# Second attention: key and query stacks without padding, 32-row score products, two heads' scores and then two maxima at a time

## The reference, cut to what matters

```
# x: (2, 1024, 128), 16 heads of width 8, causal
q, k, v = split(x @ w_qkv);  q, k = rope(q), rope(k)
scores = where(causal, q @ k.T * 8**-0.5, min)      # per head 1024 x 1024
out = softmax(scores) @ v;   return out @ w_out
```

## Time and profile before

| | |
|---|---|
| Median of 3 runs | 848.4 us (847.72 to 850.44) |
| The profiled execution: time, span of the core | 850.08 us, 848.3 us |
| TensorE matmuls busy | 778.2 us, 92% of the span |
| VectorE busy | 612.7 us |
| ScalarE busy | 506.0 us |
| GpSimd busy | 411.3 us |
| Units of the second attention, first to last score product of `scores1` | 507.7 to 812.3 us |

### The profile page before, as it was taken

The page is one execution under the profiler, slowest core; times in us unless marked ns, Lnnn a source line. Parts: engine busy times, 40 slices in busy tenths (PEclk is TensorE's granted clock), DMA queues, the critical chain, the costliest instruction groups (busy, mean ns, idle before and its releaser), DMA issues.

```text
span 848.3 us, 13857 instructions
## 1 busy us (share of the span) xinstructions
PE 778.2 (92%) x4602; PEld 455.8 (54%) x4602; DVE 612.7 (72%) x1611; ACT 506.0 (60%) x863; POOL 411.3 (48%) x466
## 2 busy tenths in 40 slices
PE   5889999999999998889999988799999999999986
PEld 2354444444444432479988864455555455564554
DVE  5878687786877797955337668777877778787554
ACT  3336665757656576345646545467776777776762
POOL 3505866667667582716060587967344132220121
PEclk9989999999999999999999998899999999999997
DMA  9210000000000000122222020000000000000001
GB/s 360 106 48 1 1 1 1 1 1 1 1 1 1 2 1 1 44 73 94 78 81 67 26 88 26 20 6 1 2 1 2 1 2 1 1 1 1 2 1 50
DMA packets 14539, 25.35 MB, mean 30 GB/s; under 512 B 3174, under 2 KB 9192, under 8 KB 14344
## 3 DMA queue, kind: packets, MB, share of 16 engines
q1 hardware_dynamic: 11798, 18.85, 6.4%
q0 software_dynamic: 2048, 4.20, 1.6%
q10 hardware_dynamic: 626, 1.43, 0.5%
HBM read 15.03 MB, written 9.44 MB: 29 GB/s over the span
## 4 chain that ended last, share of the span: by engine, by line
PE 36%; DVE 15%; POOL 6%; issue 3%; ACT 1%; DMA 0%; ACTq 0%; POOLq 0%; DVEq 0%
PE ps L1666 6%; PE ps L1751 6%; PE ps L1731 4%; DVE ps L2524 3%; PE ps L1637 3%; DVE mx_part L2527 3%; PE ps L1619 2%; PE ps L1620 2%; PE ps L1621 2%; PE ps L1629 2%; POOL xnT L658 1%; PE ps L1535 1%; PE ps L1584 1%; PE ps L1820 1%; PE ps L1759 1%
## 5 line engine op out<-in xcount | busy, mean ns | idle before, releaser
L2042 DVE TENSOR_REDUCE mx_part<-ps 128x1 f32<-128x512 f32 x256 | 163.4, 682 | 57.7 <-PE ps L1312 56.9
L1109 ACT ACTIVATE pt<-ps 128x1024 f32<-128x1024 f32 (+1 forms) x160 | 149.8, 939 | 71.8 <-PE ps L1731 70.4
L906 ACT ACTIVATE pt<-ps 128x512 f32<-128x512 f32 x256 | 140.9, 596 | 69.6 <-PE ps L1337 63.3
L1666 PE MATMUL ps<-rounded 128*128 128x128 f32 (+2 forms) x352 | 125.5, 390 | 12.4 <-DVE mx_part L2524 3.6
L2524 DVE CUSTOM_DVE_ANT_0 ps<-ps,wm 128x128 f32<-128x128 f32 (+3 forms) x256 | 119.5, 517 | 21.9 <-PE ps L1666 20.7
L1337 PE MATMUL ps<-rounded 100*128 100x512 f32 x256 | 120.8, 484 | 10.9 <-ACT pt L906 9.7
L858 ACT ACTIVATE rounded<-ps 128x512 fp32r<-128x512 f32 (+3 forms) x160 | 94.4, 592 | 57.4 <-PE ps L1301 18.3
L721 POOL TENSOR_SCALAR_AFFINE_SELECT pt<-pt 128x512 f32<-128x512 f32 x64 | 40.0, 637 | 168.1 <-ACT pt L1109 168.0
L1731 PE MATMUL ps<-rounded 128*128 128x512 f32 (+2 forms) x352 | 116.7, 372 | 0.7 <-ACT rounded L858 0.7
L1312 PE MATMUL ps<-rounded 98*128 98x512 f32 x256 | 102.5, 420 | 3.3 <-DVE mx_part L2042 3.0
L2527 DVE TENSOR_REDUCE mx_part<-ps 128x1 f32<-128x512 f32 x128 | 82.4, 685 | 28.8 <-PE ps L1666 28.5
(11 more groups left out here) (307 smaller groups left out, 1298.2 us busy)
## 6 DMA issues: line engine op xcount, KB each, us to landing
wm<-in_wm SPq DMA_DIRECT2D x1, 4896.0 KB, 16.1
to_experts<-kstage SPq DMA_DIRECT2D x6, 512.0 KB, 4.7
of_experts<-pt SPq DMA_DIRECT2D x12, 256.0 KB, 2.0
kstage<-to_experts SPq DMA_DIRECT2D x10, 256.0 KB, 2.8
wm<-in_experts SPq DMA_DIRECT2D x1, 1540.0 KB, 7.6
x<-in_x SPq DMA_DIRECT2D x4, 256.0 KB, 5.7
out<-x SPq DMA_DIRECT2D x4, 256.0 KB, 2.3
early<-in_wo ACTq DMA_DIRECT2D x1, 512.0 KB
```

Of the source, the lines that this page charges most:

```text
L906: nc.scalar.activation(pt0(k, i), ps[:, ST0_BANKS[i % 2], :], ACT.Exp, scale=SCALE0).then_inc(exp_done, 1)
L1109: nc.scalar.activation(pt[:, 4 * (t % 2) + 2 * g:4 * (t % 2) + 2 * g + 2, 0:w], ps[:, ST1_BANKS[2 * g]:ST1_BANKS[2 * g] + 2, 0:w], ACT.Exp ...
L1666: ins = mm(bank[:, o:o + w], queries1(u, i), keys[:, 0:w], start=(o == 0), stop=(o == parts[-1][1]))
L2042: v.tensor_reduce(mx_part[u % 2][:, o:o + 1], ps[:, max_bank(u, n), :], AX_X, ALU.max).then_inc(max_done, 1)
```

## The change

The key stacks lose their padding: 128 x 1024 for a unit, each head's keys in its own 32 rows, as the queries have them already. Each score product now takes 32 rows of both operands (`head_rows`), at partition 0, 32, 64 or 96. The zero fills and their semaphores go away, and four copies of 32 rows become one of 128. The order of tiles for the maxima becomes part by part and, within a part, heads 2, 3, 0, 1; and in a step two heads' scores come first, then two tiles for maxima, of the other two heads, then the next pair of each.

```diff
+HEAD_ORDER = (2, 3, 0, 1)
@@ maxima1
-        tiles += [(r, c, p) for r in range(HG) for p in parts]
+        tiles += [(r, c, p) for p in parts for r in HEAD_ORDER]
...
-        key_stack1 = [stacks[:, i * HG * S:(i + 1) * HG * S].rearrange("p (r n) -> p r n", r=HG) for i in range(2)]
+        key_stack1 = [stacks[:, i * S:(i + 1) * S] for i in range(2)]
-        first_stack = sb("first_stack", [P, HG + 1, CH], F32R)
+        first_stack = sb("first_stack", [P, 2, CH], F32R)
...
+        def head_rows(r):
+            return slice(RS * r, RS * (r + 1))
+
+        def key_piece(u, c, rows=slice(0, P)):
+            return first_stack[rows, 0, :] if u == c == 0 else key_stack1[u % 2][rows, c * CH:(c + 1) * CH]
@@ gpsimd
-            nc.gpsimd.memset(first_stack[:, 0:HG, :].bitcast(F32), 0.0).then_inc(first_zero, 1)
-            nc.gpsimd.memset(key_stack1[1].rearrange("p r n -> p (r n)").bitcast(F32), 0.0).then_inc(keys_zero[1], 1)
-                if k == 3:
-                    nc.gpsimd.memset(key_stack1[0][:, :, 0:CH].bitcast(F32), 0.0).then_inc(keys_zero[0], 1)
@@ scalar: stack_keys, in all units
-                rows = slice(RS * r, RS * (r + 1))
-                copy(key_piece(u, r, half_of(u, n))[rows], ps[rows, TURN1_BANK, :]).then_inc(stacked, 1)
+                copy(key_piece(u, half_of(u, n)), ps[:, TURN1_BANK, :]).then_inc(stacked, 1)
-            copy(key_stack1[0][:, :, CH:S], zero[:].unsqueeze(2).broadcast_to([P, HG, CH])).then_inc(half_zero, 1)
@@ tensor: scores_max1, scores1
-                    ins = mm(bank[:, o:o + w], queries1(u, i), keys[:, 0:w],
+                    ins = mm(bank[:, o:o + w], queries1(u, i, 1, rows), keys[:, 0:w],
-                             queries1(u, (c + 1) * TC - w // P, w // P), start=(o == 0), stop=(o == parts[-1][1]))
+                             queries1(u, (c + 1) * TC - w // P, w // P, rows), start=(o == 0), stop=(o == parts[-1][1]))
@@ tensor: unit1 (first_unit1 likewise)
                     for r in range(HG):
                         scores1(u, pp, r, k, False)
+                        if r % 2 == 0:
+                            continue
+                        maxima_piece(u, pp, s, k, r - 1)
                         maxima_piece(u, pp, s, k, r)
@@ vector: first_keys, four copies of 32 rows
-                v.tensor_copy(first_stack[rows, r, :], ps[rows, TURN1_BANK, :]).then_inc(stacked, 1)
+                v.tensor_copy(first_stack[:, 0, :], ps[:, TURN1_BANK, :]).then_inc(stacked, 1)
```

More of the change, by code:

```diff
@@ L190 @@
 FIRST_KEYS, FIRST_QUERIES, FIRST_MAX = 41, 43, 44
-FIRST_KEY_COPIES = {41: (0, 1), 42: (2, 3)}
+FIRST_KEYS_COPY = 41
 SECOND_TURN = {(0, 6, 1): 2, (1, 6, 0): 3}
@@ L396, in build @@
         staged, stack_turn, stacked = map(sem, ("staged", "stack_turn", "stacked"))
-        keys_zero = [sem(f"keys_zero{i}") for i in range(2)]
         stage_fixed = sem("stage_fixed")
@@ L1148, in first_unit1 @@
                         if k == g == 0:
-                            act.wait_ge(keys_zero[1], 1)
-                        if k == 0:
-                            for r in range(2):
-                                stack_keys(1, 1, 0, 2 * g + r)
+                            stack_keys(1, 1, 0)
                         if (k, g) == (1, 0):
                             stack_queries(1, 1, 0)
-                        if (k, g) in ((1, 1), (2, 0)):
-                            for r in range(2):
-                                stack_keys(1, 1, 1, 2 * (k - 1) + r)
+                        if (k, g) == (1, 1):
+                            stack_keys(1, 1, 1)
                         if (k, g) == (2, 1):
@@ L1161, in first_unit1 @@
                             stack_queries(1, 1, 1)
-                        if (k, g) in ((5, 1), (6, 0)):
-                            for r in range(2):
-                                stack_keys(2, 0, 0, 2 * (k - 5) + r)
+                        if (k, g) == (5, 1):
+                            stack_keys(2, 0, 0)
                         if (k, g) == (K1 - 1, 0):
@@ L1180, in unit1 @@
                                 stack_queries(2, 0, 0)
-                            if (k, g) in ((0, 1), (1, 0)):
-                                for r in range(2):
-                                    stack_keys(2, 0, 1, 2 * k + r)
-                        elif k in STACK1_KEYS:
-                            du, n, r = STACK1_KEYS[k]
+                            if (k, g) == (0, 1):
+                                stack_keys(2, 0, 1)
+                        elif k in STACK1_KEYS and g == 0:
+                            du, n = STACK1_KEYS[k]
                             if u + du < U1:
-                                stack_keys(u + du, (u + du) % 2, n, r + g)
+                                stack_keys(u + du, (u + du) % 2, n)
                         if k == 2 and g == 0 and s:
@@ L1213, in _ @@
             act.wait_ge(consts, N_CONST)
-            copy(key_stack1[0][:, :, CH:S], zero[:].unsqueeze(2).broadcast_to([P, HG, CH])).then_inc(half_zero, 1)
             shared_silu(3, [2])
             nc.scalar.activation(gelu_first[:], zero[0:1, :], ACT.Exp)
-            act.wait_ge(half_zero, 1)
-            for r in range(HG):
-                stack_keys(0, 0, 1, r)
+            stack_keys(0, 0, 1)
             stack_queries(0, 0, 1)
@@ L1647, in scores_max1 @@
                     pe.wait_ge(silu_done, 3 * NCH)
-                if u and c == 0 and s == MX1_FROM[u][TC, 0] + TC * r:
-                    pe.wait_ge(stacked, u * NSTACK1 + (HG + 1 + r + 1))
+                if u and s == MX1_FROM[u][TC, 0]:
+                    pe.wait_ge(stacked, u * NSTACK1 + KEYS_B)
                 if u and s == MX1_SPLIT[u]:
@@ L1663, in scores_max1 @@
                 bank = ps[:, max1_bank(u, s), :]
-                keys = key_piece(u, r, c)
+                rows = head_rows(r)
+                keys = key_piece(u, c, rows)
                 for i, o, w in parts:
-                    ins = mm(bank[:, o:o + w], queries1(u, i), keys[:, 0:w],
+                    ins = mm(bank[:, o:o + w], queries1(u, i, 1, rows), keys[:, 0:w],
                              start=(o == 0), stop=(o == parts[-1][1]))
@@ L1728, in scores1 @@
                     pe.wait_ge(exp1_done, u * (2 * K1) + (2 * (t - 1) + r // 2 + 1))
+                rows = head_rows(r)
                 for j, o, w in parts:
-                    keys = key_piece(u, r, j // TC)
+                    keys = key_piece(u, j // TC, rows)
                     ins = mm(ps[:, ST1_BANKS[r], o:o + w], keys[:, j % TC * P:(j % TC + 1) * P],
-                             queries1(u, (c + 1) * TC - w // P, w // P), start=(o == 0), stop=(o == parts[-1][1]))
+                             queries1(u, (c + 1) * TC - w // P, w // P, rows), start=(o == 0), stop=(o == parts[-1][1]))
                 if r % 2:
@@ L2507, in _ @@
                             front_qkv(t)
-                if i == FIRST_KEYS:
-                    dve.wait_ge(first_zero, 1)
-                for r in FIRST_KEY_COPIES.get(i, ()):
-                    first_keys(r)
+                if i == FIRST_KEYS_COPY:
+                    first_keys()
                 if i == FIRST_QUERIES:
```

50 lines of the change are left out of this document (24 added, 26 removed).

## The result

The changed kernel takes 891.4 us (median of 4 runs, 886.92 to 909.06), against 848.5 for the kernel before on the same chip: 1.0485 times as long, with an interval of 1.0426 to 1.0543. I had said 835. The profiled execution has a span of 892.3 us, 44.0 more than before.

The account below looks back on a forecast made before the run. A ring of two banks, VectorE's reduction and the value products was taken as the bound. 1.6 us a unit over some 6.5 units (10) plus edges 3.5 gave 13.5 off: median 848.4 to 835 us, range 822 to 858.

Parts of the forecast that it names:

- The ring: Second attention: two banks, VectorE's reduction and the value products limit a step; 3.51 us before, 3.33 forecast after.
- Steps k = 4 to 7: The four dense steps of a unit in the second attention; forecast to gain 0.7 us a unit together.
- a: Time from a step's first score product to its first tile for maxima: 0.33 us before, 0.1 assumed with overlap.
- the second pair: Third and fourth tiles for maxima in a step; forecast that a single tile stands alone for the second reduction.
- The other six steps: Steps k = 8, 9 and 0 to 3 of a unit: 20.9 us forecast against 21.8, a gain of 0.9.
- The edges: GpSimd's dropped zero fills in the first unit and VectorE's fewer key copies: 3.5 us gained (1 to 6).
- the granted clock stays full in the units behind the first: Forecast sign in the second attention: TensorE keeps full clock after the first unit, as before the change.
- rival 2: TensorE waits longer and its clock falls: 1.4 us more a step, 865 us at a third of 65 steps; chance 0.09.
- Rival 1: Row groups don't overlap for fp32r products, leaving the order alone: dense step 3.79 us, total 855; chance 0.17.
- Rival 3: Overlap comes, but changes of kind or uneven tile order eat its gain; edges remain: 846 to 850 us; chance 0.12.
- a change of kind: TensorE switching between kinds of product, such as 32-row products and full turns: 0.1 to 0.2 us each.
- the light half: The milder part of the clock-fall case, which the forecast range up to 858 us took in.

Follow-up runs that it names:

- the run that isolates it: Changed kernel with every score product over all 128 rows, so products cannot overlap and only the new order remains: 856.2 us, ratio 1.0105.
- the run with one row group: Changed kernel with every score product on rows 0 to 31, whichever head it is for, so products run one behind the other: 1021.7 us, ratio 1.199.

## Why the prediction was wrong

**The ring: right.** Steps k = 4 to 7: forecast 3.33, measured 3.33. Overlap of row groups for fp32r: there. The terms are a little off, and that their sum agrees to 0.01 is in part luck: a is 0.01 and not 0.1, from the first tile to VectorE's start it is 0.57 and not 0.43 (693.01 - 692.44), from there to the values 1.77 and not 1.83. VectorE's idle time: forecast 0.75, measured 0.76. Only the picture of the second pair was a little off: its tiles stand behind a wait of 0.58 as two records from 693.75 on, not one alone.

**The other six steps: right in sum within 0.3.** Where the clock is full the changed kernel shows, from scores to scores:

```profile
702.40 0.45 PE L1724 MATMUL ps<-rounded 32*128 32x384 f32 x2
...
706.87 0.38 PE L1724 MATMUL ps<-rounded 32*128 32x256 f32 x2
...
709.69 0.50 PE L1724 MATMUL ps<-rounded 32*128 32x512 f32 x2
...
712.70 0.44 PE L1724 MATMUL ps<-rounded 32*128 32x384 f32 x2
```

k = 8 is 4.47 (forecast 4.4), k = 9 is 2.82 (2.9), k = 0 is 3.01 (2.9). The other three are never all at full clock in the changed kernel; with the two fills, in a unit at full clock from 702.60 us on, k = 1 is 4.08 (3.9), k = 2 is 3.26 (3.2), k = 3 is 3.51 (3.6). The sum is 21.15 against 20.9. With the four dense steps (3.33 and three of 3.32) a unit put together in this way takes 34.45 against 35.8 before: a gain of 1.35 and not 1.6.

**The edges: mis-sized.** Forecast 3.5 us (1 to 6), measured 0 (ratio 1.0004). GpSimd is spared 5.3 us of fills, and the wait of 1.88 did shrink in the changed kernel, to 0.26, but TensorE comes 6 us later there (556.12 for 550.22). Where the saved time stops is not shown.

**The step that failed: "the granted clock stays full in the units behind the first", and with it rival 2 at 0.09.** I asked how long TensorE stands still, found that no wait exceeds one reduction and a bit, and that the value products fill a third of each step, and left it there. The runs show that this was the wrong question. The same order and waits with 128-row products keep the clock at 0.98; 32-row products lose it even behind 16 us in which TensorE was busy 15.90; fills of 128 rows bring it back (0.937) and equal fills of 32 rows do not (0.867). The change took three quarters of the rows out of eight products a step, and that was in the diff. In place of full clock behind the first unit the runs showed half clock for 194 of the 320 us from 520 to 840. The rival's price was right: 1.4 us a step forecast, 1.43 measured. Its extent was not: I priced a third of the steps; three fifths of 520 to 840 us were at half, from the first unit on.

**Rival 1's size** was right in the run that isolates it (3.79 and 855 forecast, 3.74 and 857 measured). **Rival 3** is there in part: a change of kind costs 0.19, as estimated (0.1 to 0.2), and part of it is inside the 1.35.

The range ended at 858, since "the light half" of rival 2 was all that it took in. With what the earlier trace rows showed, half clock in the first unit already before the change, a rival that gives TensorE less to do deserved several times its chance.

## What to carry to other kernels

Row groups make four 32-row products as quick as one and a half, but they also take rows off its products, and here the granted clock fell with them: read PEclk first after such a change, and look at products that the diff doesn't touch (here the values, 496 to 655 ns). Where TensorE already waits for another engine, faster products on it are worth only the little that lies on the ring (1.35 us of 35.8), and the fall of the clock made the program 44 us longer all the same. Useless full-row products placed in TensorE's own waits cost nothing in the dense steps at full clock (3.33 us with and without them) and held it for most of the stage. On the ring they cost 0.42 us a step, and strewn between 32-row products 0.19 us for each change of kind.

## What the runs showed that I had not expected

- With 32-row products the granted clock fell behind 16 us in which TensorE was busy 15.90, and it stood at 0.50 with TensorE busy in 40.00 of 40 us (the run with one row group, near 657 and from 680 to 720 us).
- Adding two products of 128 rows x 512 columns to each step made the changed kernel 26 us faster; adding two of 32 rows did not (865.5 and 901.4 us).
- Half clock lasts very differently within one program: in the changed kernel from about 628 to 686 us without a break, a unit and a half, and in the three units behind that only some 10 us each, after which the clock rises again. What decides which of the two comes is open.
- Moving the value products by half a step left the step where it was: 3.51 us in the kernel before, 3.33 in the changed one at full clock.
